# Second-layer sums of a graph network: register addresses in pairs and ahead of the waits, waits on sums once per pair of steps

## The reference

```python
x0_i = leaky(x0 @ W1 + b1)
x0_j = leaky(x0 @ W2 + b2)
a1 = x0_i @ wa1 + ba1[0]
a2 = x0_j @ wa2 + ba2[0]
att = jax.nn.sigmoid(a1[row] + a2[col])
msg = att[:, None] * x0_j[col]
out = jax.ops.segment_sum(msg, row, num_segments=n)
return out + x0
```

## Time and profile before

| | us |
|---|---|
| median of 3 runs | 6959.23 (6958.45 to 6972.85) |
| profiled execution | 6949.19 |
| its span, first to last instruction | 6947.4 |
| POOL's first and last gather of the second layer | 4584.9, 6841.9 |
| mean granted TensorE clock over the span | 0.770 |

### The profile page before, as it was taken

How to read it: one execution, slowest core, us unless ns; L and a number is a source line. 1 busy time by engine, 2 the same in 40 slices (tenths; PEclk the granted TensorE clock), 3 DMA queues, 4 the chain that set the end, 5 groups by cost and what they waited for, 6 DMA issues and landing times. The chain is left out here.

```text
span 6947.4 us, 76698 instructions
## 1 busy us (share of the span) xinstructions
PE 4539.0 (65%) x16367; PEld 3185.0 (46%) x16367; DVE 4423.0 (64%) x9005; ACT 2772.4 (40%) x6174; POOL 4284.4 (62%) x4006
## 2 busy tenths in 40 slices
PE   9766776667667565637888879965555555555553
PEld 5555555555555444425666654433333333333331
DVE  8766776767767555576777778954444444444447
ACT  2233333333333333328888866732222222222223
POOL 0066766767767655518788755556666666666662
PEclk9867677776777677769999999976676777676766
DMA  4388998989899888826777653345555555555554
GB/s 147 118 283 292 292 294 295 294 290 298 290 299 293 292 281 275 278 66 218 223 223 222 223 160 100 103 120 140 141 143 139 141 142 139 142 142 140 142 140 133
DMA packets 920948, 1405.60 MB, mean 202 GB/s; under 512 B 92203, under 2 KB 697635, under 8 KB 920185
## 3 DMA queue, kind: packets, MB, share of 16 engines
q0 software_dynamic: 208288, 644.62, 30.0%
q1 hardware_dynamic: 645305, 640.62, 29.3%
q10 hardware_dynamic: 66914, 115.46, 5.5%
HBM read 1127.23 MB, written 273.11 MB: 202 GB/s over the span
## 5 line engine op out<-in xcount | busy, mean ns | idle before, releaser
L676 POOL DMA_INDIRECT s_rows<-kv_rows,other x1664 | 1749.5, 1051 | 893.4 <-issue 488.6
L1434 POOL DMA_INDIRECT t_rows<-xj_rows,other x1564 | 1492.6, 954 | 781.8 <-issue 443.1
L1526 PE MATMUL ps_xsum<-t_rows,t_att 128*128 x3328 | 1208.6, 523 | 1060.4 <-DVE t_att L1487 644.0
L1526 PEld LDWEIGHTS ps_xsum<-t_rows,t_att 128*128 128x128 f32 x3328 | 807.0, 261 | 1462.3 <-issue 1326.4
L1466 ACT ACTIVATE t_att<-t_att,t_rows 128x128 f32<-128x128 f32 x1664 | 562.4, 392 | 1689.0 <-issue 1177.4
L1487 DVE SCALAR_TENSOR_TENSOR t_att<-iota,local,t_att 128x128 f32<-128x128 f32 x1664 | 579.0, 348 | 978.8 <-ACT t_att L1466 491.7
L787 PE MATMUL ps_q<-node_tab,hot 128*128 x3328 | 1154.0, 503 | 45.0 <-issue 44.1
L785 PE MATMUL ps_rel<-rel,hot 64*128 64x64 f32 x3328 | 590.9, 332 | 853.0 <-DVE s_rows L768 587.0
L765 DVE TENSOR_TENSOR s_rows<-s_rows,ps_rel 128x1024 f32<-128x1024 f32 x416 | 506.2, 1217 | 886.8 <-remote 699.4
L785 PEld LDWEIGHTS ps_rel<-rel,hot 64*128 64x128 f32 x3328 | 531.9, 240 | 1045.1 <-issue 902.3
L692 ACT ACTIVATE hot<-apart,ones 128x1024 f32<-128x1024 bf16 x416 | 477.7, 1148 | 1241.6 <-remote 756.9
(11 more groups left out here) (218 smaller groups left out, 3559.4 us busy)
## 6 DMA issues: line engine op xcount, KB each, us to landing
v_edges<-s_rows SPq DMA_DIRECT2D x416, 512.0 KB
a_terms<-v_edges SPq DMA_DIRECT2D x416, 512.0 KB, 4.4
apart<-what_rows SPq DMA_DIRECT2D x416, 256.0 KB
t_att<-a_rows ACTq DMA_DIRECT2D x416, 256.0 KB
s_rows<-kv_rows,other POOLq DMA_INDIRECT x1664
t_rows<-xj_rows,other POOLq DMA_INDIRECT x1564
kv_rows<-kv_out SPq DMA_DIRECT2D x97, 256.0 KB, 2.0
xj_rows<-n_hx SPq DMA_DIRECT2D x97, 130.0 KB, 2.4
```

What stands on the lines that cost most here:

```text
L676: pool.indirect_dma_start(out=rows[g % KV_RING][:, k, :], out_offset=None, in_=t["kv_rows"], in_offset=bass.IndirectOffsetOnAxis(ap=t["oth ...
L1434: pool.indirect_dma_start(out=rows[:, at:at + XW], out_offset=None, in_=t["xj_rows"], in_offset=bass.IndirectOffsetOnAxis(ap=t["other1"][: ...
L1526: nc.tensor.matmul(ps_sum[g % 4][:, k, :], att[g % ATT_RING][:, k, :], rows[:, bass.ds(slot[k] * XW, D)], start=True, stop=True)\
```

## The change

On DVE, PE and ACT the four addresses of a group are now formed right behind the load of the register values, ahead of the group's waits; lower_ap emits the register operations there, and those that stand next to each other are merged into fused instructions of two addresses. On DVE the wait for PE's sums is written for even steps alone; on PE the wait for the adds too, and it now stands ahead of the wait for the weighing. The values waited for are the same as before.

```diff
--- before.py
+++ after.py
@@ -1459,12 +1459,14 @@
                     load_a1(g + LEAD)
                 at = g % QUARTER
                 need = act.value_load(needs[g // QUARTER * 32:g // QUARTER * 32 + 1, at:at + 1], min_val=1, max_val=TG)
-                slot = slots_of(nc, act, slots, g)
+                a2 = [rows[:, bass.ds(slot * XW + D, 1)] for slot in slots_of(nc, act, slots, g)]
+                for column in a2:
+                    act.lower_ap(column)
                 act.wait_ge(a1_in[g % ATT_RING], 16 * (g // ATT_RING + 1))
                 act.wait_ge(landed, need)
                 for k in range(U):
                     last = nc.scalar.activation(att[g % ATT_RING][:, k, :], att[g % ATT_RING][:, k, :], ACT.Sigmoid,
-                                                bias=rows[:, bass.ds(slot[k] * XW + D, 1)])
+                                                bias=a2[k])
                 last.then_inc(att_ready, 1)
 
         @block.vector
@@ -1487,21 +1489,27 @@
                 dve.scalar_tensor_tensor(w, t["iota"][:, :], t["local1"][:, g * U + k:g * U + k + 1], w, ALU.is_equal, ALU.mult)\
                     .then_inc(hot_att_ready, 1)
 
-            def add(g, k, block):
-                acc = tab[:, bass.ds(block * AW, D)]
-                dve.wait_ge(summed, g * U + k - k % 2 + 2)
+            def sums_of(g):
+                sums = [tab[:, bass.ds(block * AW, D)] for block in blocks_of(nc, dve, t["places1"], g)]
+                for acc in sums:
+                    dve.lower_ap(acc)
+                return sums
+
+            def add(g, k, acc):
+                if k % 2 == 0:
+                    dve.wait_ge(summed, g * U + k + 2)
                 if g * U + k:
                     dve.wait_ge(added, g * U + k)
                 dve.tensor_tensor(acc, acc, ps_sum[g % 4][:, k, :], ALU.add).then_inc(added, 1)
 
             for g in range(G + 3):
                 if g >= 3:
-                    blocks = blocks_of(nc, dve, t["places1"], g - 3)
+                    sums = sums_of(g - 3)
                 for k in range(U):
                     if g < G:
                         weigh(g, k)
                     if g >= 3:
-                        add(g - 3, k, blocks[k])
+                        add(g - 3, k, sums[k])
             dve.wait_ge(added, G * U)
 
         @block.tensor
@@ -1518,12 +1526,14 @@
             pe.wait_ge(ends_set, 1)
             pe.wait_ge(slots_set, 1)
             for g in range(G):
-                slot = slots_of(nc, pe, slots, g)
+                xj = [rows[:, bass.ds(slot * XW, D)] for slot in slots_of(nc, pe, slots, g)]
+                for row in xj:
+                    pe.lower_ap(row)
                 for k in range(U):
+                    if g >= 4 and k % 2 == 0:
+                        pe.wait_ge(added, (g - 4) * U + k + 2)
                     pe.wait_ge(hot_att_ready, g * U + k + 1)
-                    if g >= 4:
-                        pe.wait_ge(added, (g - 4) * U + k - k % 2 + 2)
-                    nc.tensor.matmul(ps_sum[g % 4][:, k, :], att[g % ATT_RING][:, k, :], rows[:, bass.ds(slot[k] * XW, D)], start=True, stop=True)\
+                    nc.tensor.matmul(ps_sum[g % 4][:, k, :], att[g % ATT_RING][:, k, :], xj[k], start=True, stop=True)\
                         .then_inc(summed, 1)
```

## The result

The changed kernel takes 6936.99 us at the median (6917.51 to 6942.69, 8 runs) beside 6958.42 us for the kernel before (8 runs). The ratio is 0.9965, its 95% interval 0.9954 to 0.9977: 16 to 32 us faster, where 76 us were forecast. The profiled execution took 6941.45 us, 7.7 us less than that of before.

The account below looks back on a forecast made before the run. POOL's gathers and its 322.3 us of waits for SP were taken to bound the second layer's sums; 6949.2 less 76 gave 6873 us, plus 10.0 for the median 6883 us, range 6760 to 6995 us.

Parts of the forecast that it names:

- The bound: Second layer's sums: POOL's gathers set the length; only its 322.3 us of waits for SP can be shortened.
- The term of 76 us: POOL's waits for SP: shrink with the instructions removed, 50 to 102 us, middle taken as 76 us.
- The outer bound: POOL's waits: nothing gained if slow stretches come from its gathers alone; as the no-change rival 6959 us, 20%.
- rival N: Follow-up rival, second layer's sums: gain goes with sequencer instructions removed, about 9 us DVE, 8 PE, 4 ACT; no chance given.
- Rival 1: Second layer's sums: slow instructions vanish and all 322 us of POOL's waits go, 6637 us; chance 12%.
- Rival 3: Head of each DVE group: address block delays the first weighing in catch-ups, 43 to 66 us slower, about 7009 us; chance 18%.
- The rule on recording: Whole kernel: recording instructions can throttle engines, so unrecorded runs would be up to 322 us shorter; kept only for no change.
- The range and its sign: Whole kernel's time: 6760 to 6995 us for 8 in 10, with faster at 0.60.

Follow-up runs that it names:

- a_dve: Kernel before with DVE's part of the change alone (addresses ahead of waits, one wait on sums per pair); ratio 0.9992 to the kernel before.
- a_addr: Changed kernel with waits written for every step on DVE and PE and PE's two waits in old order; ratio 0.9989 to the kernel before.
- d_pool: Changed kernel with POOL itself waiting for PE's count of sums, against constants; 6985.02 us beside 7009.81 for the kernel before, ratio 0.9960.
- f_noa1: Changed kernel without the loads of scores behind the first eight groups, ACT waiting for sums instead; 6935.16 us, ratio 0.9972 to the kernel before.

## Why the prediction was wrong

- **The bound.** Right: POOL's line sets the stage's length, and nothing but its waits for SP could shrink. The counts of instructions came out as said on DVE and PE, and the waits got fewer rather than shorter, as said. On ACT half of the forecast instructions went, so 3735 and not 4152; that is a small part of the miss. The sentence "it is the lateness of ACT, DVE and PE that holds POOL" was wrong.
- **The term of 76 us.** This is the step that failed: "If POOL's waits go with the number of all instructions, 322.3 x 0.155 = 50 us go. If they go with the number of sequencer instructions [...] 322.3 x 0.316 = 102 us." The waits fell by 15.8 us, 5% for 14.0% fewer instructions (28% of the sequencer ones), and the last gather began 5.2 us earlier where 75 were forecast. The price was put on the wrong cause. I took the lateness of ACT, DVE and PE from the idle times and the 700 ns instructions. The trace of before already spoke against it, had I set the end of each needed sum beside SP's release: PE was 12 us ahead of what SP saw. What the runs show in place of the term is that PE's sums are counted late, 11.9 us on average, whoever waits, and that POOL's waits end about when its gathers have landed. The slow instructions and the late count are both there on the first kind of chip and both absent on the second. Slow instructions of DVE, PE and SP can go with POOL's waits left at 300 us (changed kernel, a_dve, a_addr, d_pool), so they do not make the late count. Whether both have one cause stays open; that DVE's slow instructions came back as waits for its own count speaks for it, though f_noa1 had neither.
- **The outer bound** "nothing, if the stretches come from POOL's gathers alone" was the one nearest to the truth and had 20%. The waits end about when the gathers have run out; that the gathers are the cause is argued from this and not shown. The gain itself, 14 waits fewer with the single one longer, is in line with chains that catch up faster after each release, and with rival N at a fifth of the forecast price. That is argued; the parts are too small to show it.
- **Rival 1** expected the crawl to vanish with the waits. On two of four engines the slow instructions vanished, and POOL's waits did not. **Rival 3** (DVE's address block) did not happen here: the two merged instructions cost 93 ns each, 0.19 us a group, inside the bounds of 0.11 to 0.30. It may be what the second kind of chip shows; that was not tested.
- **The rule on recording** was set aside on the ground that unrecorded runs were no shorter. It would have made the lateness a matter of the recording. The runs on the second kind, recorded the same way, have none of it, so recording alone does not make it. That it has no part in it on the first kind is not shown: a fifth to a quarter of the updates of PE's count have no record there, and every timed run on record has a granted clock, so none is known to have run with nothing recorded.
- **The range and its sign.** The sign was right and 6937 us lies within 6760 to 6995, but that is owed to the width of the range and not to the sum. The range did not foresee a chip on which the same program takes 6213 us. Nothing in one profile tells that, and the forecast should have said that it holds for a chip like the profiled one.

## What to carry to other kernels

When an engine waits for a count, find in the trace when the last operation that the count needs ended, and compare it with the release; if the gap is many microseconds, the work upstream is not late, and making it shorter or leaner buys next to nothing. When a kind of slow instruction vanishes, look whether its time did: forming register addresses ahead of the waits is cheap (93 ns for two on DVE) and ended DVE's slow instructions, but DVE then stood 261 us in waits for its own count, where the instructions had cost about 223. Measure a change worth a few tenths of a per cent on more than one chip, since here its gain was not there on the other kind.

## What was not expected of the hardware

- One program took 6952 to 7010 us on some chips and 6213 to 6219 us on others. In the profiles of the changed kernel (6939.6 and 6223.6 us) 695.5 of the 716.0 us of difference lie in the two stages with indirect gathers: 2648.7 beside 2220.6 us, and 2242.4 beside 1975.0. The granted clock differs too (0.766 and 0.815), but POOL, which sets the pace of the second, takes 0.95 us for a gather on both.
- On the slower ones, held gathers of POOL began 11.6 to 17.5 us on average after the end of the sum that they needed (6.8 to 31.5 us in single cases), and the updates of PE's count came in bursts once POOL had stood still. DVE's count of weighings reached a PE that was ready for it in 0.04 us at the median; over 0.5 us passed in 3 of 669 cases in the kernel before, and in 49 of 478 in the changed one.
- On the same chips register, load, assertion and semaphore instructions take about 700 or 1400 ns in some stretches, where their medians are 17 to 342. On DVE and PE this ended with the addresses formed ahead of the waits, on ACT it did not. In the kernel before every register instruction of DVE and PE in this stage carries a wait; whether that, or its place right behind a wait, is what matters was not tried.
